# Cross-attention mask written into the score buffers by ScalarE, and a third score buffer, in a fused decoder layer

## What is computed

```python
x = x + _L0_attn_ref(_layernorm(x), Wqa, Wqb, Wkva, Wkvb, Wout, bout)   # causal, 16 heads of 16, 4 key heads
x = x + _L0_xattn_ref(_layernorm(x), ctx_1024, ctx_1024, mask, ...)     # 16 heads, every token against ctx
x = x + _L0_ffn_ref(_layernorm(x), w1, b1, w2, b2)                      # hidden 1024, relu, fp8 rounding
```

```python
scores = jnp.einsum('bhqd,bhkd->bhqk', query, key_h) * scale
scores = jnp.where(mask == 0, jnp.float32(-1000000000.0), scores)
attn = jax.nn.softmax(scores, axis=-1)
```

## Time and profile before

| | |
|---|---|
| median of 3 runs | 1978.36 us (1977.97 to 1979.83) |
| profiled execution, its own time | 1985.14 us |
| profiled execution, span of the trace | 1983.5 us |
| mean granted TensorE clock | 0.98 of full speed |

### The profile page before, as it was taken

How to read it: one execution, slowest core, us unless ns; L and a number is a source line. 1 busy time by engine, 2 the same in 40 slices (tenths; PEclk the granted TensorE clock), 3 DMA queues, 4 the chain that set the end, 5 groups by cost and what they waited for, 6 DMA issues and landing times.

```text
span 1983.5 us, 33931 instructions
## 1 busy us (share of the span) xinstructions
PE 1792.5 (90%) x12542; PEld 1036.3 (52%) x12542; DVE 1391.6 (70%) x2192; ACT 865.7 (44%) x1320; POOL 643.4 (32%) x698
## 2 busy tenths in 40 slices
PE   2879999999989999899999989999899999989897
PEld 1545555555545555555555545555555555545554
DVE  4668585785858768585885858768585786858662
ACT  3325344443444335344443544345344543544343
POOL 3241414324151251414324151252415324151300
PEclk9979999999999999999999999999999999999998
DMA  6370543725245270543725245270543725154230
GB/s 166 46 104 12 82 62 46 104 32 78 41 65 85 33 105 20 81 62 46 104 33 81 37 67 82 33 113 14 80 60 46 104 33 84 35 70 70 34 44 11
DMA packets 86606, 124.08 MB, mean 63 GB/s; under 512 B 10481, under 2 KB 53938, under 8 KB 86322
## 3 DMA queue, kind: packets, MB, share of 16 engines
q1 hardware_dynamic: 83650, 115.26, 41.5%
q0 software_dynamic: 2160, 7.87, 1.0%
q10 hardware_dynamic: 768, 0.57, 0.1%
HBM read 21.42 MB, written 8.39 MB: 15 GB/s over the span
## 4 chain that ended last, share of the span: by engine, by line
PE 56%; issue 19%; DVE 12%; POOL 6%; DMA 3%; ACT 2%; SPq 0%; POOLq 0%; ACTq 0%; DVEq 0%
PE small L1013 9%; PE o_ps L1174 7%; PE small L1237 6%; DVE negmax L746 5%; PE score L1139 5%; PE score L1096 5%; PE score L1101 4%; POOL P L469 3%; PE score L1066 3%; PE small L1268 3%; DVE xn L732 2%; DMA Q<-negT 2%; PE small L1284 2%; DVE negparts L757 2%; PE small L997 2%
## 5 line engine op out<-in xcount | busy, mean ns | idle before, releaser
L746 DVE TENSOR_REDUCE negmax<-score 128x4 f32<-128x1024 f32 (+1 forms) x448 | 538.8, 1222 | 124.9 <-PE score L1101 83.2
L570 ACT ACTIVATE P<-score 128x1024 f32<-128x1024 f32 x448 | 447.8, 1025 | 178.7 <-PE score L1116 105.1
L1174 PE MATMUL o_ps<-P,V 128*32 128x256 f32 (+1 forms) x4096 | 283.3, 363 | 25.1 <-POOL P L469 19.8
L781 DVE TENSOR_TENSOR P<-P,cross_bound 128x1024 f32<-128x1024 f32 x192 | 226.5, 1221 | 56.7 <-ACT P L570 50.8
L468 POOL TENSOR_TENSOR carrier<-minus_half 128x1 f32<-128x1 f32 x160 | 56.1, 351 | 644.4 <-ACT P L570 640.2
L1013 PE MATMUL small<-xnT,w 128*128 128x512 f32 x392 | 204.7, 665 | 5.2 <-ACT inT L527 2.7
L1096 PE MATMUL score<-K,Q 96*128 96x256 bf16 x1024 | 155.9, 274 | 56.3 <-issue 32.3
L1174 PEld LDWEIGHTS o_ps<-P,V 128*32 128x32 f32 x4096 | 86.4, 108 | 164.6 <-issue 72.8
L1139 PE MATMUL score<-Q,K 99*128 99x256 bf16 x1024 | 155.8, 275 | 7.5 <-DVE negmax L746 7.4
L408 POOL TENSOR_TENSOR rstd<-vareps,minus_half 128x4 f32<-128x4 f32 x48 | 55.0, 1146 | 307.3 <-DVE vareps L727 307.3
L1101 PE MATMUL score<-cross_q,identb 128*128 128x512 bf16 x512 | 154.2, 382 | 0.0
(11 more groups left out here) (141 smaller groups left out, 3034.4 us busy)
## 6 DMA issues: line engine op xcount, KB each, us to landing
Q<-q1p SPq DMA_DIRECT2D x96, 256.0 KB, 7.5
K<-k2p SPq DMA_DIRECT2D x96, 256.0 KB, 8.0
Q<-q2p SPq DMA_DIRECT2D x192, 128.0 KB, 5.0
x_in<-in_x SPq DMA_DIRECT2D x16, 512.0 KB, 7.8
ctxT<-in_ctx SPq DMA_DIRECT2D x16, 512.0 KB, 7.7
k2f<-q1f SPq DMA_DIRECT2D x32, 256.0 KB, 3.5
out_y<-x POOLq DMA_DIRECT2D x15, 512.0 KB, 4.8
K<-k1p SPq DMA_DIRECT2D x96, 64.0 KB, 7.3
```

Of the source, the lines that this page charges most:

```text
L570: A.activation(P[:, t % 4, :], score[b][:, :, :], ACT.Exp, scale=SCALE).then_inc(score_free[b], 1)
L746: V.tensor_reduce(negmax[:, k, h:h + 1024 // w], s.rearrange("p (h w) -> p h w", w=w), AX.X, ALU.max, negate=True).then_inc(score_free[b], 1)
L781: V.tensor_tensor(p, p, cross_bound[:, t % 2, :].unsqueeze(1).broadcast_to([128, 4, SEQ]), ALU.min).then_inc(probs_masked[1], 1)
L1174: last = T.matmul(o_ps[ob][32 * j:32 * j + 32, SEQ * gg + q0:SEQ * gg + SEQ], v, p, start=s == 0, stop=end, tile_position=(0, 32 * j), ski ...
```

## The change

ACT writes the mask, with a Copy of `cross_q` from SBUF (broadcast over the four heads, 1024 columns), into a score buffer before PE uses it (`premask`). PE waits for that (`masked`), and its four products of a tile accumulate onto what stands there; the two mask matmuls of a tile are gone. The two output banks become one pair, `o_pair`, which is a third score buffer in S2: tiles 0 to 11 use the buffers 0, 1, 2 in turn, and tiles 12 to 15 use 0, 1, 0, 1. The masks of tiles 0 to 2 stand in ACT's program between `values1` and the copies of `xnT2_`; those of the tiles 3 to 15 each wait for the row_max that frees their buffer, and stand among ACT's other work of the stage, whose order is kept. `cut_max` waits for the last reader of the third buffer too. E2's tiles go on in the two old buffers.

```diff
-        o_ps = [stack.enter_context(nc.psum_tensor(f"o_ps{n}", [128, 512], f32)) for n in range(2)]
+        o_pair = stack.enter_context(nc.psum_tensor("o_pair", [128, 2, 512], f32))
+        o_ps = [o_pair[:, n, :] for n in range(2)]
+        cross_bufs = [score[0], score[1], o_pair]
...
+        masked = [sem(f"masked{n}") for n in range(3)]
...
+        CROSS_BUF = [0, 1, 2] * 4 + [0, 1, 0, 1]
+        CROSS_USES = [CROSS_BUF.count(n) for n in range(3)]
...
+            def premask(g, t):
+
+                n, use = cross_use(g, t)
+                _, before = cross_tile(g, t)
+                if t == 2:
+                    for ob in range(2):
+                        act.wait_ge(o_free[ob], g * UNITS + UNITS // 2)
+                if positive(before):
+                    act.wait_ge(score_free[n], before)
+                A.activation(cross_bufs[n][:, :, :].rearrange("p c (j k) -> p (c j) k", j=2),
+                             cross_q[:, t // 4 % 2, :].unsqueeze(1).broadcast_to([128, 4, SEQ]),
+                             ACT.Copy).then_inc(masked[n], 1)
...
                     values1(st)
+                for t in range(3):
+                    premask(i, t)
                 turns(st, "xnT2_", inT)
                 if prev:
                     hidden(st, [2])
...
                 if prev:
-                    hidden(st, range(3, HT))
-                if nxt:
-                    part("q1", 0, whole, part1, i + 1)
-                    part("k1", 0, whole, part1, i + 1)
-                maxima(st, 1, 0)
-                if nxt:
-                    part("q1", 1, rest1, part2, i + 1)
-                    part("k1", 1, rest1, part2, i + 1)
-                if prev:
-                    ffn_out(st, 0)
+                    hidden(st, range(3, HT - 2))
+                for t in range(3, N2):
+                    premask(i, t)
+                    if prev and t in (5, 8):
+                        hidden(st, [HT - 2 + (t - 5) // 3])
+                    if nxt and t == 6:
+                        part("q1", 0, whole, part1, i + 1)
+                    if nxt and t == 7:
+                        part("k1", 0, whole, part1, i + 1)
+                    if t == 12:
+                        maxima(st, 1, 0)
+                    if nxt and t == 13:
+                        part("q1", 1, rest1, part2, i + 1)
+                    if nxt and t == 14:
+                        part("k1", 1, rest1, part2, i + 1)
+                    if prev and t == 14:
+                        ffn_out(st, 0)
+                if prev:
                     ffn_out(st, 1)
...
-                    n, before = tile("S2", g, t)
-                    if positive(before):
-                        pe.wait_ge(score_free[n], before)
+                    n, use = cross_use(g, t)
+                    pe.wait_ge(masked[n], use + 1)
                     for c in range(2):
                         for j in range(2):
                             h = 4 * hg + 2 * c + j
-                            T.matmul(score[n][:, c, SEQ * j:SEQ * j + SEQ],
-                                     Q2[0:KROWS, b, h, 128 * (k % 2):128 * (k % 2) + 128],
-                                     K2[0:KROWS, h, SEQ * b:SEQ * b + SEQ], start=j == 0, stop=False,
-                                     skip_group_check=True)
-                    for c in range(2):
-                        last = T.matmul(score[n][:, c, :], identb[:, :],
-                                        again(cross_q[:, k % 2, :], 2), start=False, stop=True,
-                                        skip_group_check=True)
+                            last = T.matmul(cross_bufs[n][:, c, SEQ * j:SEQ * j + SEQ],
+                                            Q2[0:KROWS, b, h, 128 * (k % 2):128 * (k % 2) + 128],
+                                            K2[0:KROWS, h, SEQ * b:SEQ * b + SEQ], start=False, stop=True,
+                                            skip_group_check=True)
                     last.then_inc(score_full[n], 1)
```

More of the change, by code:

```diff
@@ L226, in layer @@
         small_free = [sem(f"small_free{n}") for n in range(2)]
-        score_full = [sem(f"score_full{n}") for n in range(2)]
-        score_free = [sem(f"score_free{n}") for n in range(2)]
+        score_full = [sem(f"score_full{n}") for n in range(3)]
+        score_free = [sem(f"score_free{n}") for n in range(3)]
+        masked = [sem(f"masked{n}") for n in range(3)]
         o_free = [sem(f"o_free{n}") for n in range(2)]
@@ L257, in layer @@
         N1, N2 = GB * 6, GB * 8
-        TILE0 = {"S1": 0, "E1": N1, "S2": 2 * N1, "E2": 2 * N1 + N2}
-        TILES = 2 * N1 + 2 * N2
+        CROSS_BUF = [0, 1, 2] * 4 + [0, 1, 0, 1]
+        CROSS_USES = [CROSS_BUF.count(n) for n in range(3)]
+        assert CROSS_USES[0] == CROSS_USES[1]
+        TILE0 = {"S1": 0, "E1": N1, "E2": 2 * N1 + 2 * CROSS_USES[0]}
+        TILES = 2 * N1 + 2 * CROSS_USES[0] + N2
         PV0 = {0: 0, 1: N1}
@@ L279, in tile, with cross_use, cross_tile @@
             return n % 2, g * (TILES // 2) + n // 2
+        def cross_use(g, t):
+            n = CROSS_BUF[t]
+            return n, g * CROSS_USES[n] + CROSS_BUF[:t].count(n)
+        def cross_tile(g, t):
+            n, use = cross_use(g, t)
+            return (n, use) if n == 2 else (n, g * (TILES // 2) + N1 + CROSS_BUF[:t].count(n))
         def o_bank(a, g, u):
@@ L562, in unit_out @@
                         act.wait_ge(small_full[st.bank(name)], st.before(name) + 1)
-                    A.activation(o_sb[:, u % 2, :], o_ps[b][:, :], ACT.Copy).then_inc(o_free[b], 1)
+                    A.activation(o_sb[:, u % 2, :], o_ps[b], ACT.Copy).then_inc(o_free[b], 1)
                 for t in range(n):
@@ L643, in _ @@
             act.wait_ge(loaded, 16 * LOADS)
+            act.wait_ge(mask_step, 7)
             def body(i, prev, nxt):
@@ L736, in row_max @@
             def row_max(a, g, t):
-                b, before = tile(("S1", "S2")[a], g, t)
+                b, before = tile("S1", g, t) if a == 0 else cross_tile(g, t)
                 dve.wait_ge(score_full[b], before + 1)
-                s = score[b][:, :, :].rearrange("p c n -> p (c n)")
+                s = cross_bufs[b][:, :, :].rearrange("p c n -> p (c n)")
                 if a == 0 and t % 6 >= 4:
@@ L749, in cut_max @@
             def cut_max(a, g, t, b):
-                for last in (t, t - 1):
-                    n, before = tile(("S1", "S2")[a], g, last)
+                for last in (t, t - 1) if a == 0 else (t, t - 1, 5 if b == 0 else 11):
+                    n, before = tile("S1", g, last) if a == 0 else cross_tile(g, last)
                     dve.wait_ge(score_free[n], before + 1)
```

## The result

The changed kernel takes 2171.5 us (median of 4 runs, 2169.1 to 2173.5) against 1979.1: a ratio of 1.0972, 95% interval 1.0953 to 1.0991. It is 192 us slower, where 28 were forecast and 53 was the end of the range.

A forecast was written before the change was run, and what follows sets the result against it. S2 was taken as level between TensorE and VectorE, VectorE ending last at 1.27 us a tile. 2.23 - 0.76 + 0.6 = +2.07 us in 14 groups, +29, less about 1: 2006 us, range 1986 to 2032.

The forecast's parts named there:

- part 2: Stage S2, from its first product to the last row maximum: -0.76 us a group, between -1.1 and +0.2.
- Part 1: Masks 0 to 2 delay ScalarE's copies, hidden tile 2, cross queries and S2: +2.23 us a group, +1.7 to +2.7.
- The price of a mask: ScalarE's write of 1024 columns to PSUM: 1.03 us to the result, 0.95 start to start, ends 0.78 and 1.12.
- Part 3: TensorE's granted clock between turns and queries, with new idle time ahead of hidden tile 2: +0.6 us a group.
- stays low through the first half of the queries: One of three ways for the granted clock ahead of S2: low into the cross queries, +1.3 us.
- The first tile: Start of S2: mask matmuls ahead of the first row maximum are gone, -0.44 us a group.
- the shorter cut_max: First cut_max in S2: about 1.15 us for 2.04 as GpSimd's subtractions end earlier, -0.9 us a group.
- The last two, in the tail: End of S2 on two buffers: VectorE waits for tiles 14 and 15, +0.43 and +0.71 us a group.
- one of 0.15: Tile 7 in S2: its mask stands behind ScalarE's other work, so VectorE waits +0.15 us a group.
- the prediction's own signs of being wrong: Masks under 0.9 us, hidden tile 2 unmoved, VectorE waits mid-S2, or 1.2 GHz for over 4 us ahead of S2.
- clock stays down: Rival: low clock through all queries and into hidden tiles, +2.6 for +0.6, 2034 us; slower by more, clock or ScalarE, 0.15.
- the change would unload what it says: Rival: TensorE bounds S2, so 7.0 us a group come back; no chance of its own, faster in all 0.08.

The follow-up runs named there:

- the seven-mask kernel: Changed kernel with three buffers throughout, q1p and k1p copies early, ScalarE writing only masks 0, 1, 2, 5, 8, 11, 14: 1914.5 us, 0.9665 of the kernel before.

## Why the prediction was wrong

**The step that failed** is one that the working did not have. The change removed 64 instructions ahead of TensorE's loop and 63 from the loop itself, and the sum put what that does to the place of the loop at nothing. It cost 133.1 - 122.9 = 10.2 us a group, 6.7 in the wait at the start of E2 and 3.4 behind it, where TensorE waits again and runs at the low clock. In time it is 2171.5 - 2037.9 = 134 of the 192 us, which agrees with 13 reloads of 10.2 us. The profile of before held a hint (19 packets on queue 8: nothing loaded in the loop), and the sum had no term for it. A second step failed too, part 2 below: even with the loop moved the kernel takes 2037.9 us, past the 2032 at the range's end.

The Trainium skill ("Runtime: NRT & Kernel Launch", Instruction fetch mechanics) says that TensorE's instruction memory is 128 KiB, 2048 instructions, a FIFO refilled in blocks of 16 KiB, and that a taken branch whose target is not in the current window of two blocks forces a fetch. The packets of 16 KB agree. The window of two blocks does not: the kernel before jumps back over 1676 instructions in each pass, and queue 8 brings it nothing there. By the figure of 2048 a loop of 1613 or of 1676 instructions fits; the runs show it kept at seven blocks and loaded anew at eight. That the nine packets of a pass are the eight blocks and one read ahead, so that eight do not stay, fits the counts, and was only argued.

**Part 1, the masks ahead of the copies**: right. +2.23 us was forecast, a wait of 2.36 us appeared in the place named, and hidden tile 2 started 2.1 us later behind the turns than before (3.45 us for 1.34). The price of a mask, too:

```profile
L632 ACT ACTIVATE score<-cross_q 128x1024 f32<-128x1024 bf16 x192 | 193.2, 1018 | 92.0 <-DVE negmax L786 90.1
```

1.02 us, for 1.03 taken, and 0.95 from start to start. The Trainium skill's faster write to PSUM ("ScalarE: Activation LUTs", Step-by-step: what each stage is for) is 0.02 us here, against the copy of as many columns within SBUF, 1.04 us, which reads fp32 where the mask reads bf16.

**Part 3, the clock**: the right direction, too small: +0.6 was taken, and the queries at 4.69 for 3.62 us and hidden tile 2 at 3.78 for 3.35 are +1.5, a little over the +1.3 of "stays low through the first half of the queries", in all 14 middle groups.

**Part 2, the stage**: -0.76 was forecast, +0.3 measured (23.3 for 23.0). The first tile and the shorter cut_max came as worked out: VectorE started 0.64 us after the first product, the cut_max took 0.94 us for the forecast 1.15. The waits did not, and the last row maximum ended 24.3 us after the first product, where the prediction had 23.3. VectorE in the kernel with the moved loop:

```profile
990.50 1.23 DVE L786 TENSOR_REDUCE negmax<-score 128x4 f32<-128x1024 f32 x1 [0.66 <-PE score L1135]
...
994.74 1.22 DVE L786 TENSOR_REDUCE negmax<-score 128x4 f32<-128x1024 f32 x1 [0.82 <-PE score L1135]
996.44 1.23 DVE L786 TENSOR_REDUCE negmax<-score 128x4 f32<-128x1024 f32 x1 [0.48 <-PE score L1135]
998.11 1.22 DVE L786 TENSOR_REDUCE negmax<-o_pair 128x4 f32<-128x1024 f32 x1 [0.44 <-PE o_pair L1135]
...
1002.23 1.22 DVE L786 TENSOR_REDUCE negmax<-score 128x4 f32<-128x1024 f32 x1 [0.63 <-PE score L1135]
1004.17 1.23 DVE L786 TENSOR_REDUCE negmax<-score 128x4 f32<-128x1024 f32 x1 [0.72 <-PE score L1135]
```

The last two, in the tail, were forecast at 0.43 and 0.71. The four before (2.4 us) had one of 0.15 against them. Two mistakes of opposite sign stand behind this. VectorE's pace was read as 1.27 us and is 1.13, so it caught up with the masks sooner; by the difference of the terms, the faster pace gave back some 1.2 us of the waits (an estimate: 0.3 + 0.43 + 0.71 + 1.10 - 3.75). And TensorE was taken to be free of the stage: with its mask matmuls gone it waited for ScalarE (1.28 and 0.85 us), and its clock fell within S2:

```profile
981.00:989.00 8.00, 6.53 (x40) 4.13 (x40) 7.26 (x7) 5.79 (x8) 0.04 (x1) 1.00 0.91 132
989.00:997.00 8.00, 6.30 (x29) 3.84 (x30) 5.93 (x9) 6.85 (x9) 3.19 (x2) 0.62 0.92 115
```

(the windows of the same kernel; the granted clock is the number 1.00, then 0.62). Its products and the quarters beside them then took 0.85 us each for 0.44. That the copies between the masks made a large part of the waits is shown by the run that moved them (30 us). Two of the prediction's own signs of being wrong had come: VectorE waited in the middle of S2, and the clock was low for over 4 us ahead of it (0.50 through the 3.57 us of hidden tile 2, 0.77 on the mean of the 4.69 us of queries).

**The sum without the code**: 4.0 us a group for 2.07, 58 us for 28. **The rival** "clock stays down" (2034 us) comes near that in time by luck, with another split: of its 2 us beyond the forecast 0.9 came in front and 1.1 in S2, where it had nothing. The rival that the change would unload what it says was put aside because of VectorE's pace; at the true pace there were 2 us more a group to be had, and the seven-mask kernel has them.

## What to carry to other kernels

Where TensorE's hardware loop has some 1600 instructions or more, count the 16 KB pieces that it touches (seven stayed here, eight did not), after every edit, also of edits ahead of the loop: adding or removing a few instructions can cost more than the edit is worth, and the instruction queue's packet count tells it. Put preparatory work (a mask, a fill) into its engine's idle time, not merely into an idle engine: in front of a copy that others wait for, 2.9 us of it cost 3.5. Take the distance between two busy rows for an engine's own pace only where the next input was long there.

## What the runs showed that was not expected

- **A loop of 1613 TensorE instructions over eight pieces is loaded whole in every pass**, nine packets of 16 KB, with a stand of 6.4 to 6.8 us at its start; a loop of 1676 over seven is loaded once. Moving the first by 96 instructions ends it; moving the second by 160 brings it about, with a stand of 5.7 to 6.2 us.
- **A small VectorE instruction beside GpSimd waits for GpSimd's instruction to end**: the cast of 32 columns takes 0.18 us alone and 0.70 or 2.02 us beside it, and all 29 such casts of the kernel before end within 0.1 us of GpSimd's instruction. The row maxima of 1024 columns keep their length beside it (1.22 us, 30 of them). One line moved on ScalarE removes one such meeting a group, and the kernel is 36 us faster.
- **Half of these 36 us are clock.** The stage got 1.4 us shorter, and the other 1.3 us of a group are the dip of the clock ahead of the queries: 12 of the 14 middle groups had it before, none of 14 with the moved line, though nothing near the dip was edited; 5 to 13 of them in the other kernels without the long wait for ScalarE. What decides on which groups it falls was not tried apart. Differences of one per cent in this kernel can come from that alone, and the sums of single gains don't add up.
- **The third buffer by itself gives 28 us**: 1.25 us a group, 17 us, in the stage, because TensorE can work ahead while VectorE is in the cut_max; the rest goes with the dip, in 6 groups in place of 12.
